# A graph layer on one core: PE adds a message's fourth tile, ACT counts more, statistics in pairs of blocks

## The reference

```python
deg = max(zeros(N).at[dst].add(1.0), 1.0)                  # N = 100000 nodes, E = 50000 edges
edge_weight = (deg[src] * deg[dst]) ** -0.5
edge_msg = relu(edge_attr @ W1e + b1e) @ W2e + b2e         # edge_attr E x 64, W1e 64 x 128, W2e 128 x 128
messages = (x[src] + edge_msg) * edge_weight[:, None]      # x N x 128
agg = segment_sum(messages, dst, N)                        # dst is sorted, and denser at low numbers
combined = (1.0 + gin_eps) * x + agg
h = relu(combined @ W1n + b1n) @ W2n + b2n
out = h + x
out = out * rsqrt(mean(out * out, -1) + RMS_EPS) * rms_w
y = layernorm(x + out)                                     # mean and variance over the 128 columns, eps 1e-5
```

## Time and profile before

| what | us |
|---|---|
| median of 3 runs | 1274.73 (1272.25 to 1275.76) |
| the profiled execution, its own time | 1275.69 |
| its span, first to last instruction | 1273.9 |
| DVE busy | 1215.2 (95%) |
| ACT busy | 1148.9 (90%) |
| PE busy | 1104.9 (87%), granted clock 0.985 of full on average |
| GpSimd busy | 998.1 (78%) |

### The profile page before, as it was taken

One profiled execution on the slowest core, in us unless ns is written; L12 is line 12 of the kernel. 1 busy time (PEld: TensorE's weight loads), 2 busy tenths in 40 slices (PEclk: granted clock), 3 DMA queues, 4 the chain that ended last, 5 costly groups with the idle time before them and its releaser, 6 DMA issues. The chain is left out here.

```text
span 1273.9 us, 31103 instructions
## 1 busy us (share of the span) xinstructions
PE 1104.9 (87%) x7488; PEld 826.9 (65%) x7600; DVE 1215.2 (95%) x4672; ACT 1148.9 (90%) x3932; POOL 998.1 (78%) x1302
## 2 busy tenths in 40 slices
PE   6898998999989999997988888788887889899992
PEld 3353567777777777775766666566565666677771
DVE  8999978999999999995999999999999999999998
ACT  7686958888989898986899999999999999999997
POOL 7787777777777777577777776777777777999997
PEclk9999999999999999998999999999999999999997
DMA  4799997666565566787668888877888776777654
GB/s 110 264 382 347 393 381 267 183 180 186 185 179 184 175 180 183 229 317 277 245 218 304 300 322 294 301 293 272 314 277 307 291 257 217 277 265 273 268 220 193
DMA packets 87739, 328.37 MB, mean 258 GB/s; under 512 B 24920, under 2 KB 28164, under 8 KB 63120
## 3 DMA queue, kind: packets, MB, share of 16 engines
q1 hardware_dynamic: 55848, 255.49, 54.4%
q0 software_dynamic: 30016, 69.49, 17.6%
q10 hardware_dynamic: 1704, 1.59, 0.4%
HBM read 180.18 MB, written 153.95 MB: 262 GB/s over the span
## 5 line engine op out<-in xcount | busy, mean ns | idle before, releaser
L743 POOL DMA_INDIRECT xs<-in_x,src_x x392 | 402.3, 1026 | 119.4 <-issue 118.1
L769 POOL DMA_INDIRECT agg_scratch<-staged,sca_i x384 | 381.0, 992 | 124.5 <-issue 114.9
L1670 PE MATMUL bank<-cT,w1n 128*128 128x512 f32 x392 | 214.3, 629 | 70.2 <-ACT cT L972 70.2
L1648 PEld LDWEIGHTS bank<-w2n,hn 128*128 128x128 f32 x1568 | 206.8, 193 | 70.6 <-issue 64.7
L990 ACT ACTIVATE squares<-res 128x128 f32<-128x128 f32 x784 | 247.6, 387 | 0.2 <-DVE res L1433 0.2
L1648 PE MATMUL bank<-w2n,hn 128*128 128x128 f32 x1568 | 207.7, 276 | 3.9 <-ACT hn L977 0.4
L1001 ACT ACTIVATE on<-z,offset,rstd 128x128 f32<-128x128 f32 x438 | 204.5, 566 | 0.5 <-DVE offset L1399 0.4
L990 ACT ACTIVATION_READ_ACCUMULATOR squares<-res 128x1 f32 x784 | 203.3, 281 | 0.0
L1567 PE MATMUL bank<-digits,picks 128*128 128x221 f16 x1568 | 186.1, 261 | 2.2 <-DVE digits L1307 2.2
L1319 DVE SCALAR_TENSOR_TENSOR picked<-iota_x,src_top,bank 128x221 f16<-128x221 f16 x392 | 171.1, 438 | 3.6 <-PE bank L1567 3.5
L1459 DVE BATCH_NORM_STATS2 stats<-z 128x6 f32<-128x128 f32 x784 | 168.8, 275 | 0.0
(11 more groups left out here) (190 smaller groups left out, 2156.1 us busy)
## 6 DMA issues: line engine op xcount, KB each, us to landing
agg_scratch<-zeros SPq DMA_DIRECT2D x48, 1024.0 KB
xn<-in_x SPq DMA_DIRECT2D x48, 1024.0 KB
out<-on SPq DMA_DIRECT2D x48, 1024.0 KB, 4.6
ag<-agg_scratch SPq DMA_DIRECT2D x47, 1024.0 KB, 6.7
staged<-sums_scratch POOLq DMA_DIRECT2D x28, 896.0 KB, 8.5
sums_scratch<-sums SPq DMA_DIRECT2D x47, 512.0 KB
highq<-src_key_scratch SPq DMA_DIRECT2D x49, 256.0 KB, 3.7
ea<-in_edge_attr SPq DMA_DIRECT2D x45, 256.0 KB
```

The costliest lines, as they stand in the source:

```text
L743: pool.indirect_dma_start(out=xs[:, b % XS, j, :], out_offset=None, in_=x, in_offset=bass.IndirectOffsetOnAxis(ap=src_x[:, t:t + 1], axis= ...
L769: pool.indirect_dma_start(out=agg_rows, out_offset=bass.IndirectOffsetOnAxis(ap=sca_i[:, t:t + 1], axis=0), in_=staged[:, k % STAGES, j, : ...
L1648: last = pe.matmul(ps[4 + s][:, j * P:(j + 1) * P], hn[:, s, j * P:(j + 1) * P], w2n[:, :], start=False, stop=j == TB - 1)
L1670: pe.matmul(ps[2 + s][:, :], w1n[:, :], cT[:, s, :], start=True, stop=True).then_inc(hn_done, 1)
```

## The change

Five things change.

1. Edge stage: DVE adds the gathered rows to three tiles of a batch only (384 columns). For the fourth, PE adds them in PSUM with one more matmul by the identity, and ACT weighs that tile straight from the bank, before the other three. A new semaphore, `last_weighed`, tells PE that the bank may be written again.
2. Counting stage: ACT makes the sign table for all four tiles of every even batch. DVE makes the fourth only in odd batches.
3. Node stage: blocks 0 to 43 take their small statistics in pairs: nine operations of 2 x 16 columns for eight steps instead of twice nine of 16. The ring of `stats` has four blocks instead of two. The lags of what follows grow: ACT's `on` from 20 steps to 21, DVE's `on` from 18 to 20, GpSimd's from 18 to 20.
4. While GpSimd takes no part, ACT makes three tiles of `on` in three steps of four and two in the fourth; DVE makes the rest.
5. `MIX_ALONE` goes from 132 to 140 and `END_ALONE` from 116 to 124. The written-out part between the loops grows; the second loop covers steps 160 to 175 only (one trip).

```diff
-    MIX_ALONE, END_ALONE = 132, 116
+    PAIRED = (BLOCKS - 4) // 2 * 2
+    MIX_ALONE, END_ALONE = 140, 124
...
+        def act_share(w):
+            return TB - 2 if w % SPB == SPB - 1 else TB - 1
...
+        def act_tiles(b):
+            return TB - b % 2
...
-                for m, w in scaled_steps(n, u, 18, 15):
+                for m, w in scaled_steps(n, u, 20, 15):
...
-                for j in range(TB - 1):
+                for j in range(act_tiles(b)):
                     act.activation(steps[:, s, j, :], iota_h[:, 0:LOW], ACT.Sign,
...
-                    for j in range(TB):
+                    act.activation(weights[:, r, TB - 1, :], ps[4 + r][:, (TB - 1) * P:W], ACT.Copy,
+                                   scale=ds[:, m // 2 % 2, r * TB + TB - 1:r * TB + TB]).then_inc(last_weighed, 1)
+                    for j in range(TB - 1):
                         last = act.activation(weights[:, r, j, :], msg[:, r, j, :], ACT.Copy,
...
-                    share = 3 if ended_alone(m) else 1 if ...
+                    share = act_share(w) if ended_alone(m) else 1 if ...
...
-                dve.tensor_tensor(msg[:, s, :, :].rearrange("p j d -> p (j d)"), ps[4 + s][:, :],
-                                  xs[:, b % XS, :, :].rearrange("p j d -> p (j d)"), ALU.add).then_inc(msg_ready, 1)
+                dve.tensor_tensor(msg[:, s, 0:TB - 1, :].rearrange("p j d -> p (j d)"), ps[4 + s][:, 0:(TB - 1) * P],
+                                  xs[:, b % XS, 0:TB - 1, :].rearrange("p j d -> p (j d)"), ALU.add).then_inc(msg_ready, 1)
...
+                if paired(n, u, 16):
+                    K, v = (n - 16) // (2 * SPB), pair_slots(u, 16)
+                    both = stats[:, v:v + 2, :, :]
+                    dve.wait_ge(stats_ready, at((K + 1) * 2 * SPB))
+                    dve.tensor_tensor(apart2[:, :, :], both[:, :, :, 1], both[:, :, :, 4], ALU.subtract)
...
                     need(pe, msg_ready, b - 2)
+                    need(pe, last_weighed, b - 2)
                     pe.matmul(ps[4 + r][:, :], ones_b[:, :], bias[:, 0, :, :].rearrange("p j d -> p (j d)"),
                               start=True, stop=False)
                     pe.wait_ge(h_ready, at(b))
                     for j in range(TB):
-                        last = pe.matmul(ps[4 + r][:, j * P:(j + 1) * P], he[:, r, j * P:(j + 1) * P], w2e[:, :],
-                                         start=False, stop=j == TB - 1)
-                    last.then_inc(m_done, 1)
+                        pe.matmul(ps[4 + r][:, j * P:(j + 1) * P], he[:, r, j * P:(j + 1) * P], w2e[:, :],
+                                  start=False, stop=False)
+                    pe.wait_ge(xs_in[(b - 1) % XS], ((b - 1) // XS + 1) * 16 * TB)
+                    pe.matmul(ps[4 + r][:, (TB - 1) * P:W], ident[:, :], xs[:, (b - 1) % XS, TB - 1, :],
+                              start=False, stop=True).then_inc(m_done, 1)
```

More of the change, by code:

```diff
@@ L444, in run_nodes @@
             unroll = SPB * XR
-            rounds = STEPS // unroll
-            first = min(MIX_ALONE + 6, END_ALONE + 16) // unroll
-            then = -(-max(MIX_ALONE + 7, END_ALONE + 20) // unroll)
+            rounds = PAIRED * SPB // unroll
+            first = min(MIX_ALONE + 6, END_ALONE + 18) // unroll
+            then = -(-max(MIX_ALONE + 8, END_ALONE + 22) // unroll)
             def written(lo, hi):
@@ L479, in ended_alone, with paired, pair_slots, single @@
             return below(m, END_ALONE)
+        def paired(n, u, lag):
+            K = (n - lag) // (2 * SPB)
+            return u % (2 * SPB) == lag % (2 * SPB) and (not isinstance(K, int) or 0 <= K < PAIRED // 2)
+        def pair_slots(u, lag):
+            return (u - lag) // (2 * SPB) % 2 * 2
+        def single(k):
+            return isinstance(k, int) and PAIRED <= k < BLOCKS and not late(k)
+        def act_share(w):
+            return TB - 2 if w % SPB == SPB - 1 else TB - 1
         def late(B):
@@ L518, in count_bank, with act_tiles_by @@
             return ps[COUNTS[(2 * b + j // 2) % 3]][:, j % 2 * (W // 2):j % 2 * (W // 2) + COLS]
+        def act_tiles(b):
+            return TB - b % 2
+        def act_tiles_by(b):
+            return sum(act_tiles(k) for k in range(b))
         DST_DMAS = G + 2
@@ L978, in node_step @@
                 k, c = (n - 16) // SPB, ((u - 16) // SPB) % 4
-                if u % SPB == 0 and live(k, BLOCKS) and not late(k):
+                if u % SPB == 0 and single(k):
                     root_variance(k, c)
+                if paired(n, u, 18):
+                    K = (n - 18) // (2 * SPB)
+                    act.wait_ge(variance_ready, at(K * 2 + 2))
+                    need(act, rstd_ready, K * 2)
+                    act.activation(spread[:, :, :].rearrange("p b i -> p (b i)"), variance[:, :, :].rearrange("p b i -> p (b i)"),
+                                   ACT.Sqrt, bias=ln_eps[:, 0:1], scale=1.0 / D).then_inc(spread_ready, 2)
                 k, c = (n - 14) // SPB, ((u - 14) // SPB) % 4
@@ L1422, in chain @@
                 k, c = (n - lag) // SPB, ((u - lag) // SPB) % 4
[L1423 removed]
+                if u % SPB == phase and (single(k) or late(k) and k < BLOCKS) and late(k) == of_late:
                     operation(k, c)
@@ L1464, in node_step @@
                 chain(n, u, 15, 3, False, set_variance)
+                if paired(n, u, 16):
+                    K, v = (n - 16) // (2 * SPB), pair_slots(u, 16)
+                    dve.wait_ge(parts_ready, at(K * 2 + 2))
+                    dve.scalar_tensor_tensor(between[:, :, :], apart2[:, :, :], 32.0, apart2[:, :, :],
+                                             ALU.mult, ALU.mult).then_inc(between_ready, 2)
+                    need(dve, fin_ready, (K * 2 - 2) * SPB)
+                    dve.tensor_scalar(neg_mean[:, v:v + 2, :], mean2[:, :, :], -0.5, None, ALU.mult
+                                      ).then_inc(mean_ready, 2)
+                if paired(n, u, 17):
+                    K, v = (n - 17) // (2 * SPB), pair_slots(u, 17)
+                    dve.wait_ge(total_ready, at(K * 2 + 2))
+                    need(dve, spread_ready, K * 2)
+                    dve.scalar_tensor_tensor(variance[:, :, :], ssq[:, v:v + 2, :], LN_EPS, total[:, :, :],
+                                             ALU.mult, ALU.add).then_inc(variance_ready, 2)
+                if paired(n, u, 19):
+                    K, v = (n - 19) // (2 * SPB), pair_slots(u, 19)
+                    dve.wait_ge(spread_ready, at(K * 2 + 2))
+                    need(dve, fin_last, (K * 2 - 2) * SPB)
+                    dve.reciprocal(rstd[:, v:v + 2, :], spread[:, :, :]).then_inc(rstd_ready, 2)
                 k, c = (n - 17) // SPB, ((u - 17) // SPB) % 4
-                if u % SPB == 1 and live(k, BLOCKS) and not late(k):
+                if u % SPB == 1 and single(k):
                     invert_spread(k, c)
@@ L1470, in node_step @@
                 k, c = (n - 18) // SPB, ((u - 18) // SPB) % 4
-                if u % SPB == 2 and live(k, BLOCKS) and not late(k) and not (isinstance(k, int) and k == BLOCKS - 3):
+                if u % SPB == 2 and single(k) and k != BLOCKS - 3:
                     set_offset(k, c)
@@ L1494, in node_step @@
                 chain(n, u, 12, 0, True, sum_parts)
-                m, v = n - 18, (u - 18) % ZR
+                if paired(n, u, 16):
+                    K = (n - 16) // (2 * SPB)
+                    dve.wait_ge(between_ready, at(K * 2 + 2))
+                    dve.tensor_tensor(total[:, :, :], between[:, :, :], within[:, :, :], ALU.add).then_inc(total_ready, 2)
+                m, v = n - 20, (u - 20) % ZR
                 if live(m, STEPS) and ended_alone(m):
@@ L1501, in node_step @@
                         need(dve, out_sent[o], B // OR * 16)
-                    dve.tensor_scalar(on[:, o, h, :], z[:, v, 0, :], neg_mean[:, v // SPB, h:h + 1],
-                                      rstd[:, v // SPB, h:h + 1], ALU.add, ALU.mult).then_inc(fin_ready, 1)
+                    for j in range(TB - act_share(v)):
+                        last = dve.tensor_scalar(on[:, o, h + j, :], z[:, v, j, :], neg_mean[:, v // SPB, h + j:h + j + 1],
+                                                 rstd[:, v // SPB, h + j:h + j + 1], ALU.add, ALU.mult)
+                    last.then_inc(fin_ready, 1)
                 m, v = n - 16, (u - 16) % ZR
```

34 lines of the change are left out of this document (21 added, 13 removed).

## The result

| what | before | after |
|---|---|---|
| median, us | 1275.24 (1272.25 to 1277.3) | 1297.58 (1295.04 to 1298.76) |
| ratio after / before | | 1.0171, 95% interval 1.0152 to 1.0191 |
| span of the profiled execution | 1273.9 | 1297.0 |

The changed kernel is 22.3 us slower; 6 us were predicted, with a range that ended at 1289. The sign and the place were right, the size of one term, the new loop of the edge stage, was not.

What follows compares the result with a forecast made beforehand. No engine alone bound it: DVE in the counting and edge stages, ACT with DVE close behind in the node stage. Counting -6, edge +20, node -9, GpSimd +1 gave +6 on 1274.73: 1281 us, range 1256 to 1289.

Steps and rivals of the forecast that it cites:

- the new loop of the edge stage: Edge stage: PE waits for ACT's weighing, closing a loop of mean 4.31 us a batch against 4.09; 20 us more.
- Counting: Counting stage: DVE drops a 0.19 us operation in 49 of 98 batches; 6 us saved, bounds 0 and 9.3.
- DVE's saving in the edge stage: Edge stage: DVE's sum 0.13 us shorter, DVE at 3.96 a batch; 10 to 13 us saved if that were all.
- the rival: Edge stage: the loop over ACT does not bind, DVE's saving is gained; 1250, or 1260 with PE's matmul; chance 0.25.
- PE waiting for the gathered rows: Edge stage: PE now waits for gathered rows one step before DVE does; costed at nothing.
- Node shares and statistics: Node stage: ACT gives DVE one of twelve on operations, paired statistics save DVE time; 9 us saved, bounds 5 and 14.
- GpSimd at 140/124: Node stage: eight more steps before GpSimd joins; 1.2 us more, with GpSimd idle some 30 us.
- The one on the worse side: Edge stage: weighing slower, 0.39 instead of 0.26, and PE restarting slowly; edge +28, sum +14, 1289; chance 0.12.
- The loop returns: Node stage, first loop: its shorter body might end DVE's four issue waits, gaining another 8 us, 1273; chance 0.11.

Runs made afterwards that it cites:

- e10: Changed kernel without its edge part and without its counting part (ACT makes three tiles' sign tables in every batch, as before): 1266.3 us.
- e13: Kernel before with DVE's message sum cut from 512 to 384 columns and nothing in its place (ACT weighs the third tile twice): 1275.7 us.
- e14: Kernel before with ACT's root, ds and weighing put ahead of he in its step instead of behind it: 1272.3 us.
- e11: Kernel before with one thing changed, GpSimd taking part from steps 140 and 124: 1277.6 us.
- e12: Changed kernel with one thing undone, GpSimd taking part from steps 132 and 116 as before: 1293.6 us.
- e3: Changed kernel with ACT doing root, ds and the fourth tile's weighing ahead of he, the other three tiles behind it: 1273.1 us.
- e5: Kernel before with only the fourth tile weighed first and PE's bias matmul waiting for that weighing of two batches before: 1290.8 us.

## Why the prediction was right or wrong

*Counting: right.* -6 predicted, 5.1 in the trace, 5.7 by e10.

*DVE's saving in the edge stage: size right, worth wrong.* The sum went from 0.69 to 0.55 us, and in e13 it takes 0.46 from start to start, as predicted. "DVE sets that" was right: its sums came every 4.09 us, and e14, with the loop relieved, stays there. But the gain of 10 to 13 us in the rival was never there: 3.99 as the next bound left out the joined batches, with which the loop stands at 4.06, so that some 0.03 x 90 = 3 us could be had. This did not spoil the main term, which counted the new loop as a whole.

*The new loop: right in kind, too small.* This is the step that failed: 4.00 and 4.62 us summed, 4.19 and 4.81 measured from `h` to `h`, against a base of 4.09. Term by term:

| term | predicted | measured |
|---|---|---|
| `h` to `he`, `he` | 0.75 + 0.73 | 0.75 + 0.73 |
| weighing one tile from PSUM | 0.26 | 0.37 |
| ACT's end to PE's weight load | 0.05 | 0.11 |
| weight load to w2e | 0.31 | 0.24 |
| w2e, the new matmul | 0.89 + 0.22 | 0.89 + 0.23 |
| half of the picks, to `h` | 0.79 | 0.87 |

Two errors make it. The weighing was priced by `joined`, the nearest row in shape and memory, though the one in hand was that of the present weighing (0.39 from SBUF, its starts 0.30 apart): the two forms differ by the scale that is read per partition, and a wait is for the end of an operation, not for the next start. The Trainium skill, "ScalarE: Activation LUTs", section "What ACT_TABLE_LOAD costs", says that each per-partition pointer operand adds about 93 ns to an ACTIVATE; the trace agrees, 0.367 against 0.264 us for the same tile from the same memory, 0.10 apart; no run here changes the scale operand alone. The picks were priced by their weight loads, 0.79, where the last two rows of the same group had the answer: 222.51 - 221.62 = 0.89 from their first matmul to `h`. The three small differences between cancel. Together 0.19 a batch too little, times 96 batches 18 us, and the edge stage comes to +39 instead of +20.

*PE waiting for the gathered rows: right*, no such wait shows.

*Node shares and statistics: right in total.* 9 predicted, between 5 and 14; steps 16 to 134 gained 13.0. Something of the node part was costed at nothing and cost 2: from the last `res` to the end the kernels with it take 23.3 to 24.3 us, those without it 21.3 to 21.8. That this is the longer distances is likely, and no run separates them.

*GpSimd at 140/124: small, as predicted.* +1 predicted (with 52 x 2.83 = 147.2, where the text has 147.4, it is +1.0); 2.6 alone (e11), 4 with the late node stage (e12), neither clear of no change. GpSimd stood idle 38.6 us where some 30 were expected.

*The rivals.* The loop binds, so 1250 or 1260 fell. The one on the worse side named one of the two mis-sizings (the weighing, 0.37 measured) and still stopped at 1289. It counted 28 us, 0.30 a batch, where the prediction's own price for 0.39 was 0.35 a batch and 32 us; that would have made +18 and 1293, outside the stated range. The rest is the picks. The loop returns stall as before: in steps 16 to 134 before, four steps of 5.0 to 5.6 us stood among steps of 3.56; in the changed kernel five of 4.9 to 7.5 stand among steps of 3.36, at the same places. The largest of them, as DVE's timeline shows it:

```profile
835.36 0.69 DVE L1468 TENSOR_TENSOR res<-bank,xn 128x512 f32<-128x512 f32 x1 [3.92 <-PE bank L1724]
```

The sum with the measured terms: -5 + 39 - 13 + 2 and small ones is +23.1, the difference of the two spans.

The best version met on the way is e1, the change without its edge part: 1260.6 us, 1.1% faster than before.

## What to carry to other kernels

Before pricing an engine's saving, take the next bound as a mean over all batches, the rare long ones included: the medians of the loop said 3.99 and its mean was 4.06, against 4.09 on the full engine. An alternating period doesn't say who sets the pace; ACT's alternated here while DVE's was even, and only relieving one and then the other (e13, e14) told which bound lay where. When a buffer's release is moved to another engine, write down the loop from start to start and price each term to the end that is waited for, from a row of the same form, scale operand included. And how much work to give an engine that comes free at a fixed time depends on when the others arrive there: eight steps gained 11 us in one kernel and seem to lose 3 or 4 in two neighbours of it, so it is set last.

## What the runs showed that was not expected

GpSimd's timetable is nearly rigid. Its 392 gathers follow one another every 1.257 us in the median, and its last scatter begins between 1067 and 1075 us in 14 of the 16 kernels here, whether the edges end at 569 or at 612. The exceptions are e3 (1084.5) and e13 (1080.0). The gathers between 250 and 500 us, of before, e13 and e3 in this order (ns least, median, most; first and last start):

```profile
L743 POOL DMA_INDIRECT xs<-in_x,src_x x199: 947/952/982, 249.8 to 499.2; - x199
```

```profile
L743 POOL DMA_INDIRECT xs<-in_x,src_x x197: 947/952/1091, 249.7 to 499.1; - x197
```

```profile
L770 POOL DMA_INDIRECT xs<-in_x,src_x x192: 947/974/1078, 249.9 to 499.0; - x192
```

In the ten kernels in which DVE sums 512 columns there are 199 gathers in this stretch, once 198 (e5) and once 200; in the six with 384 columns 196 to 198, and 192 in e3, where DVE also runs the fastest batch. e13 changes nothing in DVE's work but those columns, which points to the shorter sum as what takes about 1% of GpSimd's pace. It is one profile of each kernel, and by which way is open. The Trainium skill, "DMA: Bandwidth & Descriptors", section "SWDGE vs HWDGE vs iDMA", says that GpSimd writes its descriptor rings into SBUF, from which VectorE's two-port mode shuts it out; no run here separates that from other causes.
